# Two-layer graph network, attention layer: zero matmuls on TensorE behind each group's opening matmul, transposes over two PSUM banks instead of three

## The chip, the cores and the metric

The kernel runs on one core of a Trainium2 chip. The core has TensorE (PE; its weight loads are listed as PEld), VectorE (DVE), ScalarE (ACT), GpSimd (POOL) and SyncE (SP), each with its own instruction stream. The streams meet at semaphores. The metric is the time of one execution on the device in microseconds. Profiles are of one execution, taken by the hardware profiler.

## The reference, cut to what matters

There are 6250 nodes with 16 features and 206250 edges sorted by target node, each with 16 edge features and one of 230 types. Layer 0 is a relational message layer with hyperbolic maps. Layer 1, the attention layer, is the one that the change touches:

```python
w_m = (efeat @ W_msg + b_msg).reshape(E, in_f, -1)     # E x 16 x 16
w_a = (efeat @ W_attn + b_attn).reshape(E, in_f, -1)
h_src = feat[src][:, :, None]
e1 = w_m * h_src
e2 = w_a * h_src
seg_max = jax.ops.segment_max(e2, dst, num_segments=N)
ex = jnp.exp(e2 - seg_max[dst])
denom = jax.ops.segment_sum(ex, dst, num_segments=N)
attn = ex / denom[dst]
ft = jax.ops.segment_sum(e1 * attn, dst, num_segments=N)
return ft.sum(axis=1)
```

All matrices and sums are in float32. Edge features and weights are split into three bfloat16 parts, so that one bfloat16 matmul with a contraction over 100 rows gives a float32 product.

## The kernel before, in words

**Windows.** Nodes are ordered by degree and laid out 128 to a group, one node to a partition. A group with nodes of more than 48 edges takes several windows. Each window holds up to `S` = 48 edge slots for each of its 128 nodes. There are 50 windows here, run two at a time in a loop (`for q in range(2)`). A text that says "group" means one such pass. A window has up to eight blocks of `BLK` = 6 slots, and each block two halves of `HALF` = 3 slots. `nh` is the number of halves that a window really has, `nb` that of its blocks. Later windows have fewer.

**One window, engine by engine.** Work of window k and k+1 overlaps.

- GpSimd gathers the source features h by indirect DMAs (L325), one for each slot. For window k+1 it also fetches the edge features, and makes the second and third bfloat16 part of them (`residue`, L376; `last_part`, L380).
- TensorE, score phase: `weights(0, ...)` (L490) multiplies transposed edge features `efT` by the attention weights into one of two halves of `psW`. Between these, `exp_sums` (L496) adds the exponentials of the window before into the left half of the bank `psS`. `close_sums` (L504) ends the accumulation of the window before.
- TensorE, middle: the first two halves of the message weights, then `transposes(k + 1)` (L484): 48 transposes of edge features in six batches of 8, each batch into one bank of `psT`, which ScalarE copies to `efT` (`copies`, L620). A batch waits until ScalarE has copied the batch that used its bank before. Then TensorE waits until VectorE has read the sums of the window before (`sum_read`), and opens the new sums with a matmul of zeros of 1 row x 512 columns (L529).
- TensorE, message phase: `weights(IO, ...)` (L490) for halves 2 and later, and per block, when VectorE has put the products into `stage` (`q_ready`), `prod_sums` (L501) and a closing zero matmul (L542) that frees the ring slot (`q_free`, a ring of 3).
- VectorE, score phase: `scores(b)` multiplies `psW` by the gathered h (L1049, output in `arena`) and keeps the running maximum (L1061, L1065, L1068), then reduces it (L1070). Then `finish` for the window before: it reads `psS` (L1011), releases it, takes the reciprocal (L1013) and writes the output row (L1017).
- VectorE, message phase: `messages(b)` subtracts the maximum (L1089), multiplies the message weights in `psW` by h (L1049, output in `stage`), waits for ScalarE's exponential of the block (L637, L641), and multiplies the two (L1099).
- ScalarE: splits the edge features (L611, L614), makes the six copies of window k+1 (L620), one small exponential (L633), and the exponentials of the blocks of window k (L637), in this order.

The order on each engine is written out by hand. There is no planner. `psW` fills four PSUM banks, `psS` one, `psT` three. The third bank of `psT` (its columns 8 to 11 of 12) is also used once by the plan of windows ahead of layer 1, and by the transposes of layer 0 at the start (L430), which keep three banks.

Of the kernel before, what the change touches and what calls it, by code (L numbers as in the profile page):

```python
# [19 lines left out]
GP = 128  # L20
# [5 lines left out]
S = BLK * NBW  # L26
# [10 lines left out]
KE = 6 * D + 4  # L37
HI, MID, LO = 0, 3 * D, 5 * D
RING = 3
# [17 lines left out]
def build(nc, x, src, dst, efeat, etype, relw, loopw, relemb, wmsg, bmsg, wattn, battn, out, scratch):  # L57
    table_d, srcp_d, pairp_d, efp_d, h2_d, first_d, info_d = scratch
    ctx = ExitStack()
    with ctx:  # L60
        def sb(name, shape, dt=F32):
            return ctx.enter_context(nc.sbuf_tensor(name, shape, dt))

        def sem(name):
            return ctx.enter_context(nc.semaphore(name))
# [35 lines left out]
        efs = stage[0:GP, o2:o2 + S * KE // 2].bitcast(BF16).rearrange("p (s k) -> p s k", k=KE)  # L101
        o2 += S * KE // 2
        efT = stage[0:KE, o2:o2 + S * GP].bitcast(BF16).rearrange("k (q s n) -> k q s n", q=2, n=GP)
# [39 lines left out]
        identb = sb("identb", [128, 128], BF16)  # L143
        tri = sb("tri", [PN, PN])
        ones = sb("ones", [GP, GP])
        zero = sb("zero", [1, 512], BF16)
# [39 lines left out]
        psW = ctx.enter_context(nc.psum_tensor("psW", [128, 2, 1024], F32))  # L186
        psS = ctx.enter_context(nc.psum_tensor("psS", [128, 512], F32))
        psT = ctx.enter_context(nc.psum_tensor("psT", [128, 12, 128], F32))
        psTb = psT[:, :, :].rearrange("p a n -> p (a n)").bitcast(BF16).rearrange("p (t s n) -> p t s n", t=3, n=128)

        names = ("x_in dst_in edges_in relw_in wts_in wzero pads_ready const var_ready std_ready htan_ready hT_ps hT_sb "
# [9 lines left out]
        m = {n: sem("s_" + n) for n in names}  # L201
# [11 lines left out]
        def window(eng, k):  # L213
            v = eng.value_load(tabgn[:, ds(k, 1)], min_val=0, max_val=GC * GSTEP + GSTEP - 1)
            return v // GSTEP, (v % GSTEP) // 4 + 1
# [5 lines left out]
        def blocks(nh):  # L221
            return (nh + 1) // 2
# [48 lines left out]
        def _(pool):  # L271
# [57 lines left out]
            with pool.Fori(0, pairs) as i:  # L329
                for q in range(2):  # L330
                    k = 2 * i + q
                    _, ns = window_slots(pool, k)
                    pool.wait_ge(m["blk_in"], 16 * k + 16)
                    pool.wait_ge(m["l0_math"], k + 1)
                    pool.sem_inc(m["passed"], 1)
                    for b in range(MINS):
                        gather(table_d, blkidx, q, b, 1, tgath)
                    if q:
                        pool.wait_ge(tgath[0], pool.snap(cum[0]) * 16)
                        pool.sem_inc(m["passed"], 1)  # L340
                    else:
                        with pool.If(i > 0):
                            pool.wait_ge(tgath[1], pool.snap(cum[1]) * 16)
                            pool.sem_inc(m["passed"], 1)
                    pair_block(k + 1, 1 - q)
                    with ExitStack() as deeper:
                        for b in range(MINS, S):
                            deeper.enter_context(pool.If(ns > b))
                            gather(table_d, blkidx, q, b, 1, tgath)
                    pool.reg_add(cum[q], cum[q], ns)  # L350
# [72 lines left out]
        def _(pe):  # L423
            pe.wait_ge(m["const"], 2)
            pe.wait_ge(m["htan_ready"], 1)
            for t in range((C + 7) // 8):
                if t >= 3:
                    pe.wait_ge(m["hT_sb"], t - 2)
                for j in range(min(8, C - 8 * t)):
                    last = nc.tensor.transpose(psTb[0:KT, t % 3, j, 0:PN], htan6[:, 8 * t + j, :, :].rearrange("p j k -> p (j k)"),  # L430
                                               identb[0:PN, 0:PN])
# [32 lines left out]
            with pe.Fori(0, nstep) as t:  # L464
                pe.wait_ge(m["win_hot"], t + 1)
                for j, rhs in ((0, winhot), (1, winhot), (2, winrel)):
                    last = nc.tensor.matmul(psT[0:GP, 4 * j:4 * j + 4, :].rearrange("p a n -> p (a n)"), lhs[:, j, :],
                                            rhs, start=True, stop=True)
# [9 lines left out]
            def transposes(w):  # L478
                pe.wait_ge(m["lo_done"], w + 1)
                pe.wait_ge(m["valid_in"], w + 1)  # L480
                for t in range(S // 8):
                    pe.wait_ge(m["efT_sb"], w * (S // 8) + (t + 1))
                    for j in range(8):
                        last = nc.tensor.transpose(psTb[0:KE, t % 3, j, 0:GP], efs[:, 8 * t + j, :], identb[0:GP, 0:GP])  # L484
                    last.then_inc(m["efT_ps"], 1)

            def weights(c0, q, h, at0):
                pe.wait_ge(m["w_free"], at0 + (h + 1))
                for j in range(HALF):
                    last = nc.tensor.matmul(psW[0:GP, h % 2, j * IO:(j + 1) * IO], efT[:, q, h * HALF + j, 0:GP],  # L490
                                            wst[:, c0:c0 + IO], start=True, stop=True)
                last.then_inc(m["w_ready"], 1)

            def exp_sums(q, h):
                for s in range(h * HALF, (h + 1) * HALF):
                    nc.tensor.matmul(psS[0:GP, 0:IO], ident[0:GP, 0:GP], score[:, q, s, :], start=False, stop=False)  # L496

            def prod_sums(h):
                for s in range(HALF):
                    c0 = (h % (2 * RING) * HALF + s) * IO  # L500
                    nc.tensor.matmul(psS[0:GP, IO:2 * IO], ident[0:GP, 0:GP], prod[:, c0:c0 + IO], start=False, stop=False)  # L501

            def close_sums():
                nc.tensor.matmul(psS[0:GP, :], zero[:, 0:GP], zero[:], start=False, stop=True).then_inc(m["sum_done"], 1)  # L504

            transposes(0)
            with pe.Fori(0, pairs) as i:
                for q in range(2):
                    k = 2 * i + q
                    _, nh = window(pe, k)  # L510
                    nb = blocks(nh)
                    tb, prev = pe.snap(cumb), pe.snap(nhp)
                    pe.wait_ge(m["efT_sb"], k * (S // 8) + (S // 8 + 3))

                    for h in range(NHW):
                        if h < MINH:
                            weights(0, q, h, tb * 4)
                        else:
                            with pe.If(nh > h):
                                weights(0, q, h, tb * 4)  # L520
                        with pe.If(prev > h):
                            exp_sums(1 - q, h)
                    with pe.If(prev > 0):
                        close_sums()
                    for h in range(2):
                        weights(IO, q, h, tb * 4 + nb * 2)
                    transposes(k + 1)
                    pe.wait_ge(m["sum_read"], k + 1)
                    nc.tensor.matmul(psS[0:GP, :], zero[:, 0:GP], zero[:], start=True, stop=False)  # L529
                    for b in range(NBW):  # L530
                        for h in range(2 * b + 2, min(2 * b + 4, NHW)):
                            if h < MINH:
                                weights(IO, q, h, tb * 4 + nb * 2)
                            else:
                                with pe.If(nh > h):
                                    weights(IO, q, h, tb * 4 + nb * 2)
                        with pe.If(nb > b):
                            pe.wait_ge(m["q_ready"], tb + (b + 1))
                            prod_sums(2 * b)
                            with pe.If(nh > 2 * b + 1):  # L540
                                prod_sums(2 * b + 1)
                            nc.tensor.matmul(psS[0:GP, IO:2 * IO], zero[:, 0:GP], zero[:, 0:IO], start=False,  # L542
                                             stop=False).then_inc(m["q_free"], 1)
                    pe.reg_add(cumb, cumb, nb)
                    pe.reg_mov(nhp, nh)
            prev = pe.snap(nhp)
            for h in range(NHW):
                with pe.If(prev > h):
                    exp_sums(1, h)
            close_sums()  # L550


        @block.scalar
        def _(act):
# [8 lines left out]
            for t in range((C + 7) // 8):  # L563
                n = min(8, C - 8 * t)
# [26 lines left out]
            with act.Fori(0, pairs) as i:  # L591
                for q in range(2):
                    k = 2 * i + q
# [23 lines left out]
            def copies(w, q):  # L617
                for t in range(S // 8):
                    act.wait_ge(m["efT_ps"], w * (S // 8) + (t + 1))
                    nc.scalar.copy(efT[:, q, 8 * t:8 * t + 8, 0:GP], psTb[0:KE, t % 3, :, 0:GP]).then_inc(m["efT_sb"], 1)  # L620

            split(0)
            copies(0, 0)
            with act.Fori(0, pairs) as i:
                for q in range(2):
                    k = 2 * i + q
                    split(k + 1)
                    copies(k + 1, 1 - q)
                    _, nh = window(act, k)
# [16 lines left out]
        def _(dve):  # L646
            V = nc.vector

            for name, n in (("tbl_sb", 2), ("l0_math", 2), ("h_free", 2), ("efT_sb", 3), ("w_free", 2), ("q_free", RING),
                            ("sum_read", 1)):  # L650
                dve.sem_inc(m[name], n)
            V.memset(relW[:, RO:RO + D], 0.0)
# [215 lines left out]
            start = info[:, :, 2 * D]  # L868
# [18 lines left out]
            with dve.Fori(0, pairs) as i:  # L887
                for q in range(2):
                    k = 2 * i + q
# [138 lines left out]
            with dve.Fori(0, pairs) as i:  # L1028
                for q in range(2):
                    k = 2 * i + q  # L1030
# [3 lines left out]
                    last, odd = (nh - 1) // 2, nh % 2  # L1034
# [100 lines left out]
```

## Time and profile before

| | us |
|---|---|
| median of 3 runs (lowest to highest) | 6593.14 (6592.74 to 6606.66) |
| profiled execution | 6588.29 |
| its span, first to last instruction | 6586.6 |

Busy time over the span: TensorE 2729.8 us (41%), its weight loads 1922.8 us (29%), VectorE 3678.9 us (56%), ScalarE 1293.7 us (20%), GpSimd 4382.1 us (67%). Mean granted TensorE clock 0.92 of full speed. These shares run over two layers with different limits: layer 0 ends near 3050 us, layer 1 takes the rest. In a row, "[0.33 <-issue]" is the idle time of the engine just before it and what ended it, where "issue" is nothing that the profile shows and "remote" is something the profile cannot name. "x6" is a number of instructions shown as one line. A name like `psW<-wst,stage` is output, arrow, inputs.

### The profile page before, as it was taken

To read this page: it belongs to the slowest core of one execution; us is meant where nothing else is said; L and a number is where in the kernel's file an instruction comes from. 1 tells how busy PE (TensorE), PEld (TensorE's weight loads), DVE (VectorE), ACT (ScalarE), POOL (GpSimd) and SP (SyncE) were. 2 spreads that over 40 slices of the span, in tenths; PEclk is the share of its full clock that TensorE was granted. 3 is DMA by queue.
4 is the path that set the end of the run, shared out by engine and by line. 5 is a ranking of instruction groups with operands and counts; after the bars stand their busy time and mean duration, and the time that the engine had idled before them with its cause. 6 is when DMAs were issued, how large, how long until landed. Compare 5 with 4: busy or idle time off the path is not lost.

```text
span 6586.6 us, 56916 instructions
## 1 busy us (share of the span) xinstructions
PE 2729.8 (41%) x13477; PEld 1922.8 (29%) x13478; DVE 3678.9 (56%) x4670; ACT 1293.7 (20%) x1247; POOL 4382.1 (67%) x3814
## 2 busy tenths in 40 slices
PE   3530000000000000000567777777777777777676
PEld 1110000000000000000445555555555555555454
DVE  8221111111112111231689989998988898888877
ACT  3530000000000000000222222222222222223222
POOL 0335676767666766656477877777777777776753
PEclk9999999999999999998788888888888888888888
DMA  5880000000000000000000000000000000000000
GB/s 164 275 263 11 6 6 6 6 6 6 6 6 6 6 6 6 6 8 11 6 10 10 12 9 9 9 9 12 9 9 12 9 12 9 12 12 9 12 11 5
DMA packets 141814, 167.76 MB, mean 25 GB/s; under 512 B 73235, under 2 KB 130056, under 8 KB 135287
## 3 DMA queue, kind: packets, MB, share of 16 engines
q0 software_dynamic: 122896, 57.46, 6.2%
q1 hardware_dynamic: 18865, 110.05, 5.2%
q8 instruction: 8, 0.13, 0.0%
q14 instruction: 13, 0.11, 0.0%
q10 hardware_dynamic: 32, 0.01, 0.0%
HBM read 71.76 MB, written 108.57 MB: 27 GB/s over the span
## 4 chain that ended last, share of the span: by engine, by line
POOL 23%; issue 18%; DVE 17%; DVEq 16%; PE 13%; DMA 4%; another core or an unknown queue 4%; POOLq 2%; ACT 1%; SPq 0%; ACTq 0%
POOL gath L325 20%; DVEq L1096 6%; PE psS L501 4%; PE psS L496 4%; DVE stage L1049 4%; PE psW L490 3%; DMA table<-arena 3%; DVEq L1057 3%; DVE arena L1049 2%; DVE work L1070 2%; DVEq L1049 1%; DVE stage L1099 1%; DVE work L673 1%; DVE work L1013 1%
## 5 line engine op out<-in xcount | busy, mean ns | idle before, releaser
L325 POOL DMA_INDIRECT gath<-h_dram,hidx x1695 | 2223.5, 1312 | 509.3 <-issue 509.1
L325 POOL DMA_INDIRECT gath<-table,blkidx x1646 | 1600.0, 972 | 505.7 <-issue 503.0
L484 PE MATMUL psT<-identb,stage 128*100 128x128 bf16 x2448 | 209.5, 255 | 2599.5 <-POOL stage L380 2569.7
L501 PE MATMUL psS<-stage,ident 128*128 128x256 f32 x3390 | 976.3, 447 | 341.8 <-DVE stage L1099 297.7
L484 PEld LDWEIGHTS psT<-identb,stage 128*100 128x100 bf16 x2448 | 190.8, 155 | 2623.9 <-POOL stage L380 2531.5
L501 PEld LDWEIGHTS psS<-stage,ident 128*128 128x128 f32 x3390 | 736.5, 225 | 534.3 <-DVE stage L1099 354.0
L496 PE MATMUL psS<-arena,ident 128*128 128x256 f32 x3390 | 830.4, 382 | 0.0
L490 PE MATMUL psW<-wst,stage 100*128 100x256 bf16 x3390 | 580.0, 292 | 472.2 <-DVE stage L1049 270.0
L673 DVE TENSOR_TENSOR work<-gath 128x768 f32<-128x768 f32 x50 | 47.9, 958 | 1154.1 <-DMA gath<-table,blkidx 1150.8
L496 PEld LDWEIGHTS psS<-arena,ident 128*128 128x128 f32 x3390 | 605.5, 191 | 70.2
L1049 DVE TENSOR_TENSOR arena<-psW,gath 128x768 f32 (+1 forms) x565 | 520.7, 952 | 173.8 <-DMA gath<-h_dram,hidx 58.2
L637 ACT ACTIVATE arena<-arena x271 | 401.9, 1483 | 1019.3 <-DVE arena L1089 989.4
L1099 DVE TENSOR_TENSOR stage<-stage,arena x294 | 498.6, 1696 | 88.7 <-issue 35.3
L620 ACT COPY stage<-psT 100x1024 bf16<-100x1024 bf16 x306 | 289.9, 1026 | 1298.8 <-PE psT L484 1213.6
L1049 DVE TENSOR_TENSOR stage<-psW,gath 128x768 f32 x565 | 513.9, 949 | 24.8 <-remote 24.8
L1089 DVE TENSOR_TENSOR arena<-arena,work 128x1536 f32 (+1 forms) x294 | 496.8, 1690 | 16.2 <-issue 16.2
L490 PEld LDWEIGHTS psW<-wst,stage 100*128 100x128 bf16 x3390 | 287.2, 101 | 725.5 <-DVE stage L1049 325.8
L595 ACT ACTIVATE work<-work 128x48 f32<-128x48 f32 x50 | 12.1, 243 | 2236.7 <-DVE work L905 2092.1
L1065 DVE TENSOR_TENSOR work<-work,arena 128x1536 f32<-128x1536 f32 x171 | 328.6, 1922 | 15.8
L874 DVE SCALAR_TENSOR_TENSOR bstf<-tabs,info 128x1 f32 (+1 forms) x103 | 21.7, 211 | 472.0 <-issue 472.0
L446 PE MATMUL psW<-stage,work 102*125 102x460 bf16 (+1 forms) x400 | 190.9, 617 | 173.1 <-ACT arena L578 141.4
L376 POOL TENSOR_TENSOR efraw<-efraw,stage 128x768 f32<-128x768 f32 x51 | 86.3, 1692 | 236.2 <-DVEq L1000 173.7
(216 smaller groups left out, 2680.3 us busy)
## 6 DMA issues: line engine op xcount, KB each, us to landing
table<-arena SPq DMA_DIRECT2D x50, 1610.0 KB
gath<-h_dram,hidx POOLq DMA_INDIRECT x1695
gath<-table,blkidx POOLq DMA_INDIRECT x1646
efp<-in_edge_attr SPq DMA_DIRECT2D x1, 12890.6 KB
table<-arena SPq DMA_DIRECT2D x50, 186.9 KB
arena<-first_dram POOLq DMA_DIRECT2D x1, 915.5 KB, 12.1
info<-info_dram POOLq DMA_DIRECT2D x2, 432.0 KB, 6.4
arena<-in_dst,rowi POOLq DMA_INDIRECT x51
```

The lines of the kernel that those rows point to most:

```text
L325: pool.indirect_dma_start(out=gath[:, q, s, :], out_offset=None, in_=rows, in_offset=bass.IndirectOffsetOnAxis(ap=idx[:, q, s:s + 1].bitca ...
L484: last = nc.tensor.transpose(psTb[0:KE, t % 3, j, 0:GP], efs[:, 8 * t + j, :], identb[0:GP, 0:GP])
L490: last = nc.tensor.matmul(psW[0:GP, h % 2, j * IO:(j + 1) * IO], efT[:, q, h * HALF + j, 0:GP], wst[:, c0:c0 + IO], start=True, stop=True)
L496: nc.tensor.matmul(psS[0:GP, 0:IO], ident[0:GP, 0:GP], score[:, q, s, :], start=False, stop=False)
L501: nc.tensor.matmul(psS[0:GP, IO:2 * IO], ident[0:GP, 0:GP], prod[:, c0:c0 + IO], start=False, stop=False)
L620: nc.scalar.copy(efT[:, q, 8 * t:8 * t + 8, 0:GP], psTb[0:KE, t % 3, :, 0:GP]).then_inc(m["efT_sb"], 1)
L637: nc.scalar.activation(v, v, ACT.Exp).then_inc(m["exp_done"], 1)
L1049: V.tensor_tensor(dst_ap.rearrange("p s (i o) -> p s i o", o=D), psW[0:GP, s, 0:HALF * IO].rearrange("p (s i o) -> p s i o", i=D, o=D), bc ...
L1065: V.tensor_tensor(macc, macc, score[:, q, ds(b * BLK, BLK), :], ALU.max)
L1089: V.tensor_tensor(blk, blk, mnew[:, q, :].unsqueeze(1).to_broadcast([GP, n, IO]), ALU.subtract).then_inc(m["sub_done"], 1)
L1096: V.drain()
L1099: V.tensor_tensor(pr, pr, blk.rearrange("p s c -> p (s c)"), ALU.mult).then_inc(m["q_ready"], 1)
```

## The change

TensorE gets a helper that writes a matmul of zeros (1 row by 128, times 1 row by 512 columns) into a spare bank n times. It is called with 12 behind the opening matmul of the sums in each window, ahead of the message phase. The spare bank is the third one of `psT`. So that it is free, the batches of transposes in layer 1 alternate between two banks instead of three, in TensorE's writes and in ScalarE's reads alike. The start value of the semaphore that counts copied batches goes from 3 to 2, and so does the constant in the wait at the head of a window, which still waits for the last copy of that window.

```diff
         psT = ctx.enter_context(nc.psum_tensor("psT", [128, 12, 128], F32))
+        spare = psT[0:GP, 8:12, :].rearrange("p a n -> p (a n)")
...
                 for t in range(S // 8):
                     pe.wait_ge(m["efT_sb"], w * (S // 8) + (t + 1))
                     for j in range(8):
-                        last = nc.tensor.transpose(psTb[0:KE, t % 3, j, 0:GP], efs[:, 8 * t + j, :], identb[0:GP, 0:GP])
+                        last = nc.tensor.transpose(psTb[0:KE, t % 2, j, 0:GP], efs[:, 8 * t + j, :], identb[0:GP, 0:GP])
                     last.then_inc(m["efT_ps"], 1)
...
+            def keep_busy(n):
+                for _ in range(n):
+                    nc.tensor.matmul(spare, zero[:, 0:GP], zero[:], start=True, stop=True)
...
-                    pe.wait_ge(m["efT_sb"], k * (S // 8) + (S // 8 + 3))
+                    pe.wait_ge(m["efT_sb"], k * (S // 8) + (S // 8 + 2))
...
                     transposes(k + 1)
                     pe.wait_ge(m["sum_read"], k + 1)
                     nc.tensor.matmul(psS[0:GP, :], zero[:, 0:GP], zero[:], start=True, stop=False)
+                    keep_busy(12)
...
-                    nc.scalar.copy(efT[:, q, 8 * t:8 * t + 8, 0:GP], psTb[0:KE, t % 3, :, 0:GP]).then_inc(m["efT_sb"], 1)
+                    nc.scalar.copy(efT[:, q, 8 * t:8 * t + 8, 0:GP], psTb[0:KE, t % 2, :, 0:GP]).then_inc(m["efT_sb"], 1)
...
-            for name, n in (("tbl_sb", 2), ("l0_math", 2), ("h_free", 2), ("efT_sb", 3), ("w_free", 2), ("q_free", RING),
+            for name, n in (("tbl_sb", 2), ("l0_math", 2), ("h_free", 2), ("efT_sb", 2), ("w_free", 2), ("q_free", RING),
```

## Rows read from the trace of the kernel before

**Rows 1.** Page, part 2: VectorE's busy tenths in 40 equal slices.

```profile
DVE  8221111111112111231689989998988898888877
```

**Rows 2.** Windows of layer 1: stretch, length, busy (count) of PE, PEld, DVE, ACT, POOL; clock, DMA.

```profile
3400.00:4900.00 1500.00, 1120.21 (x5825) 820.26 (x5824) 1347.86 (x1382) 399.81 (x329) 1171.33 (x871) 0.88 0.06 10
4900.00:6500.00 1600.00, 1170.36 (x6007) 865.65 (x6007) 1383.76 (x1496) 451.00 (x376) 1165.87 (x887) 0.84 0.07 11
```

**Rows 3.** Timeline of VectorE, one group's message phase: start us, duration us, instruction.

```profile
5036.33 1.76 DVE L1089 TENSOR_TENSOR arena<-arena,work 128x1536 f32 x1 [0.33 <-issue]
5038.01 1.82 DVE L1049 TENSOR_TENSOR stage<-psW,gath 128x768 f32 x2
5039.92 1.76 DVE L1099 TENSOR_TENSOR stage<-stage,arena  x1
...
5043.26 1.81 DVE L1049 TENSOR_TENSOR stage<-psW,gath 128x768 f32 x2
```

**Rows 4.** Timeline of TensorE in the same group.

```profile
5032.68 0.38 PE L529 MATMUL psS<-zero 1*128 1x512 bf16 x1 [1.37 <-DVEq L1012]
5039.02 1.68 PE L490 MATMUL psW<-wst,stage 100*128 100x256 bf16 x6 [5.96 <-DVE stage L1049]
5041.73 5.49 PE L501 MATMUL psS<-stage,ident 128*128 128x256 f32 x12 [1.03 <-DVE stage L1099]
...
5047.36 0.83 PE L490 MATMUL psW<-wst,stage 100*128 100x256 bf16 x6
5048.03 2.75 PE L501 MATMUL psS<-stage,ident 128*128 128x256 f32 x12
```

**Rows 5.** Windows around the same gap; the clock is third from the end.

```profile
5033.00:5039.00 6.00, 0.06 (x1) 0.00 (x0) 5.43 (x8) 2.12 (x4) 4.69 (x5) 0.54 0.05 6
5039.00:5048.00 9.00, 7.91 (x25) 5.11 (x26) 8.82 (x7) 2.21 (x2) 7.31 (x5) 0.55 0.05 5
5048.00:5067.00 19.00, 15.43 (x75) 11.27 (x73) 17.55 (x17) 7.66 (x6) 15.39 (x11) 1.00 0.05 5
```

**Rows 6.** Waits after 3400 us: who waited for whom, us in total, times, longest.

```profile
DVE arena L1049 <- PE psW L490: 53.3, 89, 2.7
...
DVE stage L1099 <- issue: 35.3, 6, 9.4
...
DVE stage L1099 <- ACT arena L637: 10.9, 6, 5.2
...
DVE stage L1049 <- remote: 3.6, 3, 2.9
```

**Rows 7.** Source line L529: duration ns min/median/max, first and last start.

```profile
L529 PE MATMUL psS<-zero x50: 384/385/605, 3162.2 to 6533.7; 1*128 1x512 bf16 x50
```

**Rows 8.** Windows around the first group's transposes in the loop.

```profile
3157.00:3160.00 3.00, 3.00 (x30) 2.87 (x31) 2.90 (x2) 1.30 (x2) 0.00 (x0) 0.57 0.00 0
3160.00:3164.00 4.00, 2.11 (x26) 1.44 (x24) 3.63 (x4) 4.00 (x5) 0.00 (x0) 1.00 0.01 4
```

**Rows 9.** Timeline of the first group: six copies, and the fifth batch of transposes.

```profile
3158.70 5.58 ACT L620 COPY stage<-psT 100x1024 bf16<-100x1024 bf16 x6 [46.02 <-PE psT L484]
...
3160.68 0.65 PE L484 MATMUL psT<-identb,stage 128*100 128x128 bf16 x8 [0.18 <-ACT stage L620]
```

**Rows 10.** Timeline of ScalarE: the first block exponential of the group of rows 3.

```profile
5038.24 1.48 ACT L637 ACTIVATE arena<-arena  x1 [2.67 <-issue]
```

**Rows 11.** Timeline of a later group, 6162 to 6196 us.

```profile
6166.03 4.81 PE L484 MATMUL psT<-identb,stage 128*100 128x128 bf16 x48 [3.38 <-POOL stage L380]
...
6174.50 1.68 PE L490 MATMUL psW<-wst,stage 100*128 100x256 bf16 x6 [3.34 <-DVE stage L1049]
...
6174.76 1.01 ACT L620 COPY stage<-psT 100x1024 bf16<-100x1024 bf16 x1 [4.76 <-remote]
...
6181.99 1.01 ACT L620 COPY stage<-psT 100x1024 bf16<-100x1024 bf16 x1 [3.27 <-remote]
...
6184.73 1.76 DVE L1099 TENSOR_TENSOR stage<-stage,arena  x1 [9.42 <-issue]
```

## The prediction, made before the changed kernel was run

> **What bounds the kernel now.** I read the page's slices first. VectorE has 1 to 3 tenths in slices 3 to 18 (counted from 0), which are layer 0, and 7 to 9 tenths from slice 20 on, which is layer 1 [rows 1]. The edit touches layer 1 alone. Next the windows of that layer: from 3400 to 4900 us VectorE is busy 1347.86 of 1500 us, TensorE 1120.21, GpSimd 1171.33, and the granted clock is 0.88; in the next 1600 us they have 1383.76, 1170.36 and 1165.87, and 0.84 [rows 2]. The clock has two levels, 2.4 and 1.2 GHz, so 0.88 means that 24% of the time is at the lower one.
>
> Then one group of nodes (window of 48 edge slots), around 5033 to 5067 us, engine by engine. VectorE starts the first message block at 5036.33 (subtract), multiplies by h at 5038.01, makes the product at 5039.92, and reaches the second block's multiply at 5043.26 [rows 3]. None of these lines has an idle time in front except 0.33 us of issue. 5043.26 - 5038.01 = 5.25 us is one block and is 1.76 + 1.82 + 1.76 us of instructions, less overlaps. TensorE in the same time: the opening matmul of the sums (L529) at 5032.68, then 5.96 us of idle, which VectorE ends by giving psW back, then weights at 5039.02 in 1.68 us and the first 12 sums in 5.49 us. The next block's weights take 0.83 and its 12 sums 2.75 us [rows 4]. The windows say why: 0.54 of the clock from 5033 to 5039, 0.55 from 5039 to 5048, 1.00 afterwards [rows 5]. That is 2 x (0.46 x 6 + 0.45 x 9) = 13.6 us at 1.2 GHz per group. TensorE pays some 3.6 us for it (0.85 + 2.74), and VectorE's 5.25 us beat doesn't change. So the question is who waits for the slow TensorE.
>
> The waits answer it. Of VectorE's waits after 3400 us, the multiplies into `stage` (message blocks) have 3.6 us in 3 waits. The multiplies into `arena` (scores, on the far side of the group) have 53.3 us in 89 waits. The product waited for the exponential: 35.3 us in 6 waits and 10.9 in 6 [rows 6]. Layer 1 is VectorE bound, and the slow clock after the gap lies beside it.
>
> **The change part by part.**
>
> (a) Twelve matmuls of zeros. L529 ran 50 times, so 50 groups, 600 matmuls of 1 x 512. The trace has none of them back to back. Upper bound: L529 alone takes 0.385 us, at worst 0.605 [rows 7], so 12 x 0.605 = 7.3 us with no overlap. Lower bound: six 256-column matmuls in 0.83 us [rows 4], where the last one ends 0.28 after its start, so (0.83 - 0.28) / 5 = 0.11 us each, 0.22 for 512 columns, 2.6 us for twelve. At 1.2 GHz that doubles to 5.3. I take 2.6, since L529's own median of 0.385 us is near its minimum of 0.384, the full clock's [rows 7]. They stand between L529 and the weights for half 2. The gap is 5.96 us [rows 4], so 2.6 and 5.3 both fit. At 7.3 the weights start 1.3 us late; they are first read at 5043.26, and now end at 5040.70, which leaves 2.6 us more. So VectorE pays 0 at all three prices. What hides it is VectorE's own tail of `finish` and the first subtract. If that cover were gone, it would be 2.6 x 50 = 130 us.
>
> (b) The clock. After the zeros an idle time of about 5.96 + 0.38 - 2.6 - 0.3 = 3.4 us is left. Idle pieces that add up to 3.6 us over 19 leave the clock at 1.00 (5048 to 5067), 6 us in one piece do not [rows 4, 5]. 3.4 in one piece lies between; I take it that the clock still falls in most groups, but some 4 us later, and comes back where it did. So 13.6 becomes about 9.5 us per group; L529 runs from 3162.2 to 6533.7 in 49 steps [rows 7], which is 68.8 us from group to group, and so the mean clock gains 0.5 x 4 / 69 = 0.03, from 0.88 and 0.84 to about 0.90 and 0.87. If it never fell, it would be +0.10. Value in time: at most the 3.6 us of `stage` waits [rows 6], and nothing below that.
>
> The row bears on a rule: in the first group the mean clock was 0.57 from 3157 to 3160, which are transposes nearly throughout, so the low level and the rise lie both in them, and 1.00 up to 3164 [rows 8]. The Trainium skill (TensorE: Matmul & The Clock Gate, Part 4: PE-mode transpose) says that the full clock doesn't engage for transposes, which don't count as busy in the same way. By that rule, which speaks against this change, the zeros would find the clock already low and cost 5.3 us a group instead of 2.6, and do little for it; the row contradicts it, since the clock rose during transposes.
>
> (c) Transposes over two banks. There are six batches of 8 a group, each copied out by ScalarE. In the first group the six copies stand in 5.58 us, thus (5.58 - 1.03) / 5 = 0.91 us apart, and the fifth batch waited 0.18 us for a copy and took 0.65 [rows 9]. With two banks a batch waits for the copy one later, so the last ends 0.9 us later. On TensorE this eats into the wait before L529, or at worst pushes it by 0.9; hidden as in (a). On ScalarE two copies take 1.82 us; one copy plus one batch is 1.03 + 0.65 + some 0.1 = 1.8 at the full clock, no loss, and 1.03 + 1.06 + 0.1 = 2.2 at half clock (batch of 8 x 0.107 plus 0.2 fill, worked out from 0.65), so 0.2 a copy, 1.0 a group. ScalarE idles 2.67 us before the first exponential [rows 10], so this is free too, except where the product already waits for the exponential: 12 times [rows 6]. 12 x 1.0 = 12 us at most; I take 5.
>
> Those twelve have an own face. Around 6174 us all 48 transposes ended by 6170.84, yet the fourth copy started 4.76 us late at 6174.76 and the sixth at 6181.99, so VectorE's product stood idle 9.42 us until 6184.73 [rows 11]. The matmuls had ended but their increments came late. With two banks the sixth batch waits for the fourth copy, that is until 6175.8, and its increment follows. Bounds for this: nothing (the increments come when they come) to one further lag of 4.8 us in each of the six long waits, 29 us. I take 3. The weights at 6174.50 [rows 11] would be up to 6 us late there, while VectorE needs them about 3.5 us after 6184.73: hidden.
>
> (d) 24 more instructions in each of two unrolled loop bodies. TensorE's first pass through new code shows only as waits that no engine ends; one bound is the 3.6 us row, the other nothing: I take 1. The start value of the copy semaphore and the wait at the group's head drop by one together; the wait is for the same copy. 0.
>
> Sum on the profiled execution: 6588.3 + 0 - 1 + 5 + 3 + 1 = 6596. The page's span is 6586.6, its run 6588.3, and the median 6593.1, 4.8 higher. I forecast the median: 6593 + 8 = 6601; as (c) takes the upper half of what is likely, I shade it to 6598.
>
> **The rivals.**
>
> Slower (late increments compound): with two banks each late copy now holds TensorE, whose next increment is late in its turn. It decides where the fourth copy is late, as in rows 11. For it: in rows 11 the copies after the fourth are late again, up to 6181.99. Against: 6 of 50 groups show it at this size. Price: the full 12 + 29 us and the zeros at 5.3 us behind: 6593 + 41 = 6634.
>
> Faster (ScalarE no longer late): late increments of this kind might belong to a TensorE at 1.2 GHz; the six weights at 6174.50 took 1.68 us, which is that level [rows 4, 11]. If a clock that holds removes them, VectorE gets back its 35.3 + 10.9 us [rows 6]: 6593 - 46 = 6547. Against: the transposes come before the zeros.
>
> Nothing happens to the clock: a matmul with one row of zeros isn't counted as work. Then (b) is 0 and the mean clock stays at 0.88 and 0.84; the time is 6593 to 6601, since nothing waits for it. The clock held throughout gives the same time.
>
> **How the numbers follow.** About 0.2% (13 us) is what can be told from no change. Forecast 0.45, the clock unchanged or held 0.13, slower rival 0.24, faster rival 0.18. The first two end within 13 us of 6593 but for a tenth of them, mostly upwards. So same 0.51, slower 0.29, faster 0.20. The range goes down to 6560 and up to 6640 to take most of both rivals; the forecast's own range is 6588 to 6612.
>
> **What would show it.** Right: groups of twelve matmuls on `psT` about 2.6 us long behind L529; VectorE's beat of 5.25 us unchanged; mean clock up by 0.02 to 0.04; copies 0.91 us apart at the full clock; the `stage` multiplies still waiting a few us in all. Wrong: waits for psW in front of the second message block (then (a) isn't hidden), the product's waits for the exponential well above 50 us or gone, or a mean step from one L529 to the next off 68.8 us by over 0.3.

## The result, and the profile after

| | before | changed |
|---|---|---|
| median of 20 runs (lowest to highest), us | 6575.64 (6555.76 to 6606.66) | 6618.9 (6582.34 to 6665.19) |
| profiled execution, us (before: the one of the first table) | 6588.29 | 6605.61 |

The ratio is 1.0063, 95% interval 1.0045 to 1.0080: the changed kernel is slower. The median of before had been 6593.14 over three runs and is 6575.64 over twenty. Measured again beside the experiments below, on a chip where the kernel before is 29 us quicker (chip B), the same changed kernel gave 1.0027 (1.0012 to 1.0042), 6558.54 against 6546.22 us. So the loss is 0.3 to 0.6%, 18 to 41 us by the two ratios.

The windows of layer 1 in the trace of the changed kernel answer to [rows 2]; the clock is third from the end:

```profile
3400.00:4900.00 1500.00, 1208.32 (x6128) 852.45 (x6126) 1355.66 (x1395) 397.68 (x323) 1179.86 (x876) 0.90 0.07 10
4900.00:6500.00 1600.00, 1269.40 (x6310) 896.66 (x6309) 1379.61 (x1500) 452.64 (x376) 1158.45 (x884) 0.85 0.06 11
```

TensorE is busier by 88 and 99 us, VectorE is as before. The clock went from 0.88 to 0.90 and from 0.84 to 0.85. One group, TensorE's timeline, answers to [rows 4]. L534 is the old L529, L506 are the zeros, L491 and L502 the old L490 and L501:

```profile
5241.61 0.38 PE L534 MATMUL psS<-zero 1*128 1x512 bf16 x1
5241.84 2.75 PE L506 MATMUL psT<-zero 1*128 1x512 bf16 x12
5247.75 1.69 PE L491 MATMUL psW<-wst,stage 100*128 100x256 bf16 x6 [3.16 <-DVE stage L1055]
5250.46 5.16 PE L502 MATMUL psS<-stage,ident 128*128 128x256 f32 x12 [1.03 <-issue]
5255.56 0.28 PE L548 MATMUL psS<-zero 1*128 1x256 bf16 x1
5255.77 0.83 PE L491 MATMUL psW<-wst,stage 100*128 100x256 bf16 x6
```

The zeros take 2.75 us and the weights behind them still wait 3.16 us for VectorE, so they don't start late. They still take 1.69 us, and the first twelve sums 5.16: the half clock is back before the messages begin. VectorE in the same group answers to [rows 3]. The second block's multiply stands at 5252.62, 5.88 us behind the first instead of 5.25:

```profile
5246.74 1.82 DVE L1055 TENSOR_TENSOR stage<-psW,gath 128x768 f32 x2
5248.65 1.76 DVE L1105 TENSOR_TENSOR stage<-stage,arena  x1
5250.32 1.75 DVE L1095 TENSOR_TENSOR arena<-arena,work 128x1536 f32 x1
5252.62 1.82 DVE L1055 TENSOR_TENSOR stage<-psW,gath 128x768 f32 x2 [0.54 <-remote]
```

Its weights had ended on TensorE at 5249.44, 3.2 us earlier. The increment that tells of them came late. The waits after 3400 us, against [rows 6], show more of this kind of wait: 22 of them for `stage` where there were 3.

```profile
DVE arena L1055 <- PE psW L491: 46.0, 75, 2.7
DVE stage L1105 <- issue: 32.2, 6, 8.0
...
DVE stage L1055 <- remote: 18.4, 22, 3.5
DVE stage L1105 <- ACT arena L643: 6.5, 6, 1.2
```

Ahead of 3400 us there is one more long one, in the second group. The sixth copy started 15.81 us late, though its transposes had ended at 3245.09, and VectorE's product stood idle 30.15 us:

```profile
3244.00 1.09 PE L485 MATMUL psT<-identb,stage 128*100 128x128 bf16 x8 [1.83 <-issue]
...
3245.42 5.32 PE L506 MATMUL psT<-zero 1*128 1x512 bf16 x12
...
3266.16 1.01 ACT L626 COPY stage<-psT 100x1024 bf16<-100x1024 bf16 x1 [15.81 <-remote]
...
3268.89 1.76 DVE L1105 TENSOR_TENSOR stage<-stage,arena  x1 [30.15 <-issue]
```

That group isn't where the two traces part, though. In the same group the kernel before has 33.8 us of such waits (12.5 for the exponential, 21.3 for `stage`), the changed kernel 37.6 (30.1 and 7.5). They part in the third group. The opening matmuls of the fourth stand 24.4 us apart (before, then changed), where those of the third stood 3.2 us apart:

```profile
3412.71 0.38 PE L529 MATMUL psS<-zero 1*128 1x512 bf16 x1 [1.50 <-DVEq L1012]
3437.11 0.38 PE L534 MATMUL psS<-zero 1*128 1x512 bf16 x1 [0.57 <-DVEq L1018]
```

In between the changed kernel waits three times for `stage`, and once for the exponential for 5.1 us. The kernel before has 1.4 us for the exponential there and no wait for `stage`:

```profile
DVE stage L1055 <- remote: 16.5, 3, 11.2
```

From there to the last opening matmul the changed kernel is 5.8 us quicker (3115.2 us against 3121.0). Its 14.8 us more of `stage` waits after 3400 us are made up by 7.3 us less for scores and 7.7 us less for the exponential. So this pair of executions differs by 17.3 us, all of it by one early group, and doesn't show a price that is paid in every group.

### The profile page after: what moved, and what is told of

Same layout as the page of the kernel before. It is cut to its first block, busy times and chain, and to the rows that moved or that the text cites. A ratio compares the mean times of both kernels' runs of the same rounds, so it can differ in the third digit from the quotient of the medians.

```text
span 6603.8 us, 58116 instructions
## 1 busy us (share of the span) xinstructions
PE 2937.5 (44%) x14077; PEld 1989.3 (30%) x14078; DVE 3676.3 (56%) x4670; ACT 1299.8 (20%) x1247; POOL 4372.0 (66%) x3814
## 4 chain that ended last, share of the span: by engine, by line
POOL 24%; issue 19%; DVEq 17%; DVE 16%; PE 13%; DMA 4%; another core or an unknown queue 3%; POOLq 2%; ACT 1%; SPq 0%; ACTq 0%
POOL gath L326 21%; DVEq L1102 6%; DVE stage L1055 4%; PE psS L502 4%; PE psS L497 4%; PE psW L491 3%; DMA table<-arena 3%; DVEq L1063 3%; DVE arena L1055 2%; DVE work L1076 2%; DVEq L1055 1%; DVE work L679 1%; DVE work L1019 1%; DVE stage L1105 1%
## 5 line engine op out<-in xcount | busy, mean ns | idle before, releaser
L485 PE MATMUL psT<-identb,stage 128*100 128x128 bf16 x2448 | 231.1, 257 | 2658.6 <-issue 2543.6
L502 PE MATMUL psS<-stage,ident 128*128 128x256 f32 x3390 | 974.5, 446 | 304.8 <-DVE stage L1105 238.9
L502 PEld LDWEIGHTS psS<-stage,ident 128*128 128x128 f32 x3390 | 735.8, 225 | 499.2 <-DVE stage L1105 291.4
L491 PE MATMUL psW<-wst,stage 100*128 100x256 bf16 x3390 | 578.0, 291 | 295.7 <-DVE arena L1055 112.7
L491 PEld LDWEIGHTS psW<-wst,stage 100*128 100x128 bf16 x3390 | 286.5, 101 | 570.2 <-DVE arena L1055 200.4
```

The source lines that it names most:

```text
L485: last = nc.tensor.transpose(psTb[0:KE, t % 2, j, 0:GP], efs[:, 8 * t + j, :], identb[0:GP, 0:GP])
```

## The experiments

Twelve kernels ran, on three chips, each beside runs of the kernel before on the same chip: e1 to e4 on chip A (before: 6548.32 us), e5 to e8 on chip B (6546.22) and e9 to e12 on chip C (6574.9). Which chip the first measurement (6575.64) was taken on isn't known.

| run | what differs | ratio to before | 95% |
|---|---|---|---|
| first measurement | the change | 1.0063 | 1.0045 to 1.0080 |
| e5 | the change, chip B | 1.0027 | 1.0012 to 1.0042 |
| e1 | two banks alone | 1.0002 | 0.9993 to 1.0011 |
| e4, e7 | two banks alone, as it turned out | 1.0005, 1.0004 | 0.9996 to 1.0014, 0.9994 to 1.0015 |
| e2 | twelve zeros alone, three banks | 1.0025 | 1.0012 to 1.0039 |
| e8 | the change, zeros of 16 columns | 1.0035 | 1.0022 to 1.0048 |
| e6 | the change, 100 rows of weights for the row of zeros | 1.0024 | 1.0015 to 1.0033 |
| e9 | code of the 12 zeros present, jumped over | 1.0025 | 0.9998 to 1.0051 |
| e3 | 24 zeros | 1.0339 | 1.0325 to 1.0354 |
| e10 | code of 24 zeros present, jumped over | 1.0266 | 1.0236 to 1.0296 |
| e11 | 36 zeros of 16 columns from a loop | 1.0623 | 1.0577 to 1.0669 |
| e12 | before, fewer closing matmuls | 1.0015 | 0.9993 to 1.0037 |

**e1_banks_only.**

```diff
-                    keep_busy(12)
```

> The change without the zero matmuls: the layer 1 transposes alternate between two banks of psT, nothing is written to the third. Theory A (late copies compound): the two banks carry the loss, so the ratio to the kernel before is 1.004 to 1.008, and ScalarE's copies show more late starts and VectorE's product (message phase) waits 15 us or more longer than the 60 us it waits before. Theory B (the zeros carry it, through increments of TensorE that arrive late or weights that start late): ratio 0.998 to 1.002. Theory C (longer code in the loop bodies): also 0.998 to 1.002, since this loop is as long as before.

Measured: 6550.45 us, 1.0002. VectorE's product waited 44.4 us for the exponential in this trace after 3200 us (65.0 in that of the kernel before), not more. Theory A falls on this chip: the two banks cost nothing that can be told.

**e2_zeros_only.**

```diff
 nc.tensor.matmul(psS[0:GP, :], zero[:, 0:GP], zero[:], start=True, stop=False)
+for _ in range(12):
+    nc.tensor.matmul(psS[0:GP, :], zero[:, 0:GP], zero[:], start=False, stop=False)
```

> Three banks for the transposes as before, and behind the opening matmul of psS in each window twelve more matmuls of zeros of 1 x 512 into psS itself, accumulating, so they need no spare bank. Theory A: ratio 0.998 to 1.002, waits of VectorE's product as before. Theory B: 1.004 to 1.008. Theory C: 1.002 to 1.006. The granted clock in layer 1 should be as in the changed kernel, 0.01 to 0.04 above the kernel before, in all three.

Measured: 6565.06 us, 1.0025, which is under B's bound of 1.004 and within C's. The whole change gives 1.0027 on chip B (e5, below). Beside the 1.0002 of e1, the zeros carry the loss on these two chips, and no compounding with the banks can be told.

**e3_change_24.**

```diff
-                    keep_busy(12)
+                    keep_busy(24)
```

> The change with 24 zero matmuls in place of 12. At the full clock they take 5.2 us, which nearly fills the gap of 6 us, so the clock should mostly hold: mean granted clock in layer 1 0.93 or more, the first twelve sums of a message block 2.75 us instead of 5.5. Theory A: ratio as the change, 1.004 to 1.008, since the banks are the same. Theory B: doubled, 1.009 to 1.016, with VectorE's multiplies into stage waiting 50 us or more longer. If a clock that holds were worth time by itself, the ratio would fall below 1.003.

Measured: 6768.4 us, 1.0339. All theories missed it, and so did the clock. The 24 zeros back to back don't hold it; it is at the lower level right through them:

```profile
3995.31 10.44 PE L506 MATMUL psT<-zero 1*128 1x512 bf16 x24
4005.69 1.46 PE L491 MATMUL psW<-wst,stage 100*128 100x256 bf16 x6
```

The windows over that stretch, with TensorE busy throughout:

```profile
3995.00:4000.00 5.00, 5.00 (x12) 1.64 (x13) 4.45 (x6) 1.44 (x3) 3.78 (x5) 0.50 0.06 6
4000.00:4006.00 6.00, 6.00 (x16) 2.01 (x15) 5.37 (x5) 1.88 (x2) 5.08 (x4) 0.50 0.04 4
```

Over 47 groups the clock fell during the zeros in 38 and was already low in 9; in none did it hold. The time went somewhere else. The page's line of instruction fetches says 224 packets, where the kernel before and the changed one have 8:

```profile
q8 instruction: 224, 3.67, 0.3%
```

TensorE's branch back to the head of the loop took 4.2 to 4.9 us in 23 passes, so every second window began late, and VectorE waited for scores (`arena`) at the cold start:

```profile
5285.76 0.82 PE L491 MATMUL psW<-wst,stage 100*128 100x256 bf16 x3 [5.57 <-issue]
```

```profile
DVE arena L1055 <- PE psW L491: 161.5, 142, 3.8
```

**e4_code_not_run** and **e7_long_code_not_run.**

```diff
-                    keep_busy(12)
+                    with pe.If(nh > 100):
+                        keep_busy(12)     # 24 in e7
```

> The change with its twelve zero matmuls under a condition that is never true, so their code lies in both loop bodies but doesn't run; two banks as in the change. Theory A: the same ratio as the two banks alone. Theory B: as the two banks alone, 0.998 to 1.002. Theory C: 1.004 to 1.008 here, and above the two banks alone by that much. The branch itself costs TensorE well under 1 us a window and lies beside VectorE.

> 24 zero matmuls as in the run with 24, but under a condition that is never true, so that only their code is there. With 24 executed, TensorE's branch back to the loop's head took 4.2 to 4.9 us in all of the 23 passes after 3400 us, and 224 instruction packets were fetched instead of 8. Theory L (the loop body no longer fits where TensorE keeps its code): the same packets and the same branch here, and a ratio of 1.02 to 1.035. Theory B (24 executed zeros in front of the message weights cost it): 1.000 to 1.002.

Measured: 6553.23 us, 1.0005, and 6551.48 us, 1.0004, with 8 packets. The bound of `nh` is known when the kernel is compiled, so I take it that the zeros weren't in either program. e7's 8 packets bear this out: the same 24 matmuls under a condition on a running count take 224 (e10, below). Both are repeats of e1, and say nothing of the code.

**e5_change_again.** The changed kernel as it is.

> The changed kernel itself, beside the others of this call on one chip. The two banks alone gave 1.0002, the zeros into psS with three banks 1.0025, the code without its execution 1.0005. Theory B (the zeros' execution costs, the banks nothing): 1.002 to 1.004, that is, part of the first measurement's 1.0063 was its chip. Theory D (zeros and two banks compound, since each late increment now holds the next transposes too): 1.005 to 1.008 again.

Measured: 6558.54 us, 1.0027: B's figure, and D falls here. The first measurement's 1.0063 lies in D's range, and beside it neither part was run alone. The profiled execution took 6545.17 us, at the low end of its runs, and has few of the late increments (9 waits for `stage`, 3.4 us), so its trace can't show where the typical run loses its 12 us.

**e6_hundred_rows.**

```diff
-                    nc.tensor.matmul(spare, zero[:, 0:GP], zero[:], start=True, stop=True)
+                    nc.tensor.matmul(spare, wst[:, 0:GP], wst[:], start=True, stop=True)
```

> The change with the twelve idle matmuls made from 100 rows of the weights (100 x 128 times 100 x 512, written to the spare bank) instead of one row of zeros; same count, same columns, same code length. With one row the clock fell while they ran back to back, 0.22 us apart before and 0.43 behind. If the clock's fall depends on how many rows of the array work, it holds through these twelve, they are 0.22 us apart in nearly all groups, and the low stretch behind the gap gets some 3 us shorter than with the change (mean clock in layer 1 up by 0.02 more). If it doesn't depend on rows or data, the spacing is as in the change. The time: within 0.2% of the change by theory B, since VectorE sets the pace; a ratio at or under 1.000 only if the half clock behind the gap is what makes the increments late.

Measured: 6559.68 us, 1.0024. The twelve ran at the full clock from first to last in 24 of 47 groups and the clock fell during them in 8, where the change in e5 has 10 and 20. In the 16 us behind the opening matmul the clock is low for some 8.3 us; with the zeros 11.2 (11.4 in e5), in the kernel before 12.5. The two banks without any zeros have 11.3 as well (e1 and e7), so the one-row zeros took nothing off the half clock: what the change shows against the kernel before, the banks alone show too. The windows of [rows 2] now read:

```profile
3400.00:4900.00 1500.00, 1212.03 (x6068) 857.52 (x6066) 1358.88 (x1383) 402.20 (x326) 1187.70 (x873) 0.90 0.07 10
4900.00:6500.00 1600.00, 1254.51 (x6346) 892.58 (x6346) 1384.78 (x1506) 452.44 (x375) 1148.36 (x874) 0.89 0.07 11
```

So rows or data matter to the clock (this run doesn't part the two), and a third less of the half clock than in the kernel before, a quarter less than with the banks alone, is worth no time.

**e8_narrow_zeros.**

```diff
-                    nc.tensor.matmul(spare, zero[:, 0:GP], zero[:], start=True, stop=True)
+                    nc.tensor.matmul(spare[:, 0:16], zero[:, 0:GP], zero[:, 0:16], start=True, stop=True)
```

> The change with twelve zero matmuls of 1 x 16 columns instead of 1 x 512: as many instructions, but under 0.7 us of TensorE's time instead of 2.6 to 5.3. If the loss comes from the number of instructions that TensorE completes (its increments late behind them), the ratio stays as for the change in this call, within 0.1%. If it comes from the time that the zeros take, it falls to 1.000 to 1.001.

Measured: 6571.26 us, 1.0035. Twelve now take 0.46 us of TensorE instead of 4.2 on average, and the loss is as large. It isn't TensorE's time that costs; it is that the instructions are there, run or only in the code (e9 tries to part these two).

**e9_code_12_skipped** and **e10_code_24_skipped.**

```diff
-                    keep_busy(12)
+                    with pe.If(tb > 5000):
+                        keep_busy(12)     # 24 in e10
```

> The change with its twelve zero matmuls under a condition on the running block count that is never true and that the compiler can't fold away, so that 24 more instructions really lie in each loop body and are jumped over. (The two earlier kernels with a condition on nh turned out to be compiled without the zeros: they are repeats of the two banks alone, at 1.0005 and 1.0004.) Theory N (TensorE completes more instructions and its increments come later): 0.999 to 1.001. Theory C (longer code): 1.002 to 1.004, as the change and the narrow zeros (1.0027, 1.0035).

> The same with 24 zero matmuls skipped. With 24 executed the ratio was 1.0339, 224 instruction packets were fetched instead of 8, and the branch back to the loop's head took 4.2 to 4.9 us. If the length of the code alone does that: 150 packets or more, the same branch times, ratio 1.015 to 1.03. If fetched code is only what runs: 8 packets and 1.000 to 1.001.

Measured: e9 6599.27 us, 1.0025 (0.9998 to 1.0051), which holds both theories and doesn't part them. Its trace has no wait for `stage` after 3400 us, like those of e4 and e7. e10 6758.7 us, 1.0266, with 224 packets and the branch at 4.3 to 5.1 us. So the length of the loop alone (with one jump a window, and on chip C) makes 2.7%, where e3 has 3.4. The trace shows the same late scores:

```profile
q8 instruction: 224, 3.67, 0.2%
```

```profile
DVE arena L1056 <- PE psW L491: 186.8, 148, 3.9
```

**e11_loop_36_narrow.**

```diff
-                    keep_busy(12)
+                    with pe.Fori(0, 6) as _z:
+                        keep_busy(6)      # of 1 x 16 columns
```

> 36 zero matmuls of 1 x 16 columns in each window, from a loop of 6 passes over 6 of them, so that only about half of the change's instructions are added to the code but three times as many run. TensorE needs some 2 to 3 us for them, less than the gap of 6 us. Theory N (number of completed instructions): 1.006 to 1.011, three times the narrow zeros' 1.0035 or at least twice. Theory C (length of the code): 1.001 to 1.002. If neither, and the loss is a matter of chance in how the streams fall, it lies between 1.000 and 1.003.

Measured: 6981.18 us, 1.0623, far above all three. 8 packets, so it isn't the fetch. The timeline of one group shows TensorE going through 31 of the 36 in 1.96 us, and then stalling with nothing to wait for in front of each further one. Over the 50 groups the first stall of more than half a microsecond comes behind 18 to 35 zeros; 17 groups have none.

```profile
5258.75 1.96 PE L506 MATMUL psT<-zero 1*128 1x16 bf16 x31
5261.48 0.17 PE L506 MATMUL psT<-zero 1*128 1x16 bf16 x1 [0.77 <-issue]
5262.93 0.17 PE L506 MATMUL psT<-zero 1*128 1x16 bf16 x1 [1.29 <-issue]
5264.38 0.17 PE L506 MATMUL psT<-zero 1*128 1x16 bf16 x1 [1.27 <-issue]
5265.80 0.17 PE L506 MATMUL psT<-zero 1*128 1x16 bf16 x1 [1.26 <-issue]
5267.23 0.17 PE L506 MATMUL psT<-zero 1*128 1x16 bf16 x1 [1.26 <-issue]
5267.97 0.58 PE L491 MATMUL psW<-wst,stage 100*128 100x256 bf16 x2 [0.57 <-issue]
5268.71 1.13 PE L491 MATMUL psW<-wst,stage 100*128 100x256 bf16 x4 [0.16 <-issue]
...
5277.85 0.96 DVE L1056 TENSOR_TENSOR stage<-psW,gath 128x768 f32 x1 [8.67 <-remote]
```

The weights ended at 5269.84 and VectorE, idle since 5269.18, could read them at 5277.85. There are 94 such waits in 47 windows:

```profile
DVE stage L1056 <- remote: 337.7, 94, 10.9
```

338 us of VectorE's waits against 406 us of added time: this is the kind of wait of the changed kernel's trace, 18 times as long. Here it comes behind 48 transposes and 36 zeros in a few us, each with a weight load. Against e8, three times as many zeros and the inner loop with its branches came in together, so this run doesn't show which of the two brings the stalls; 36 narrow zeros without a loop weren't run.

**e12_fewer_closing.**

```diff
-                                prod_sums(2 * b + 1)
-                            nc.tensor.matmul(psS[0:GP, IO:2 * IO], zero[:, 0:GP], zero[:, 0:IO], start=False,
-                                             stop=False).then_inc(m["q_free"], 1)
+                                prod_sums(2 * b + 1, free=True)    # its last matmul increments q_free
+                            with pe.If(nh < 2 * b + 2):
+                                nc.tensor.matmul(psS[0:GP, IO:2 * IO], zero[:, 0:GP], zero[:, 0:IO], start=False,
+                                                 stop=False).then_inc(m["q_free"], 1)
```

> The kernel before with fewer TensorE instructions: where a block has both halves, the zero matmul of 1 x 256 columns that closes it and frees its ring slot is left out, and the last product sum does the increment instead. Some 5 matmuls and weight loads fewer per window, one branch more per block. Theory N: the ratio falls below 1, to 0.997 to 0.9995, with fewer waits of VectorE on late increments. Theory C: 0.999 to 1.001, as the code has grown by a few branches. VectorE's beat of 5.25 us stays in both.

Measured: 6582.91 us, 1.0015 (0.9993 to 1.0037). No gain that can be told; the interval leaves theory N 0.07% at most. The kernel before had only 3 waits for `stage` after 3400 us, this one has 2, so there was hardly a late increment to free. No version here is faster than the kernel before.

**The traces side by side.** One execution each. `stage` waits are VectorE's with releaser "remote" after 3400 us. The step is the mean time from one opening matmul to the next, from the fourth to the fiftieth.

| trace | chip | `stage` waits, us | step, us |
|---|---|---|---|
| before | first measurement | 3, 3.6 | 67.85 |
| the change | first measurement | 22, 18.4 | 67.72 |
| e1, e4: two banks alone | A | 0, 0 | 67.05, 67.11 |
| e2: zeros alone | A | 4, 2.0 | 67.35 |
| e7: two banks alone | B | 0, 0 | 67.10 |
| e5: the change | B | 9, 3.4 | 67.09 |
| e6: the change, 100 rows | B | 18, 9.8 | 67.64 |
| e8: the change, narrow zeros | B | 12, 4.8 | 67.27 |

Over the 46 steps, 0.3 us is 14 us. So in e2, e6 and e8 the later groups do carry a loss of the size that the medians show (8 to 25 us against the banks alone on the same chip), and in e5's trace and in that of the first measurement they don't.

## Why the prediction was right or wrong

The time fell inside the range (6560 to 6640) but not in its likeliest case: I gave 0.51 to no change and 0.29 to slower, and it was slower both times. The forecast was 5 us over the median then known for the kernel before; measured side by side it is 41 us by the ratio, or 18 on chip B. The range took that in through the room that I had left for the rivals, not through a term of the sum. That the slower rival's price was 41 us too is luck: its banks cost nothing that can be told where they ran alone.

1. What bounds the kernel: right. VectorE's beat stays at 5.25 us where no increment is late, and e6 has a third less half clock for no gain.
2. (a) The zeros lie in TensorE's gap: right as to TensorE (2.75 us at the full clock against 2.6 foretold, 5.32 at the half, 3.96 on average in the changed kernel's trace). The step that failed is "VectorE pays 0 at all three prices": the bounds counted TensorE's time alone. What the runs showed instead: by the medians the twelve cost 12 us in e5, 25 us in e8 with a ninth of TensorE's time, and 17 us in e2 without the banks. So the price hangs on the instructions being there. Through which wait it is paid is open. Late increments for `stage`, which I had listed under (c) only, are more frequent with zeros and two banks together (9 to 22 waits) than with the banks alone (none) or in the kernel before (3). But e2 has the loss with 4 of them and 2.0 us, so they aren't all of it: against e1 on the same chip its trace has 8.8 us more for the exponential and 5.1 us more for scores, in one execution each.
3. (b) The clock: the 0.90 for the first stretch was hit, the second was 0.85 and not 0.87. The hit is luck. Another execution of the same kernel (e5) has 0.88 and 0.86, and the two banks without zeros have 0.89 and 0.86 (e1). I had the clock fall in the 3.4 us of idle left behind the zeros; in 19 of 47 groups it fell while they ran, and in e3 24 of them didn't hold it either. The third rival's premise, that one row of zeros isn't counted as work, was nearer, and its conclusion, that time doesn't care, holds by e6. [rows 8] have the clock rise within a run of transposes, and a batch of eight takes 0.65 us in [rows 9] against 1.09 at the half clock (at 3244.00 above). The Trainium skill (TensorE: Matmul & The Clock Gate, Part 4: PE-mode transpose) says that the full clock doesn't engage for transposes. These rows contradict it. They don't show that transposes alone raise it: six weight matmuls ended at 3157.81, just before the rise.
4. (c) Two banks: foretold +8 us, measured by three runs at 1.0002, 1.0005 and 1.0004, or +1 to +3 us, none of them clear of zero. The slower rival had the sign, and the late increments right in kind. That they compound with the banks shows in the number of `stage` waits (point 2) and not in the time: e2 without the banks is as slow as e5 with them. Beside the first measurement, with its larger loss, this is untested.
5. (d) Longer loop bodies: foretold 1 us, and only for the first pass. I didn't ask how much room was left. With 12 zeros the loop is still fetched once; with 24 it is fetched again in every pass for 2.7%.
6. The faster rival: nothing of it showed. The copies were as late as before: counted from the end of their transposes or of ScalarE's instruction before, 68 late starts with 119 us in all in the changed kernel's trace against 53 with 98.
7. Of the signs of being wrong one came: the mean step from one opening matmul to the next was 69.2 us, 0.4 over 68.8. From the fourth group on it was 67.7, against 67.9 in the kernel before, so this sign speaks of the third group and not of the rest.

What stays open: which waits make up the 0.3% of the twelve, and whether they come from running the zeros or from the code's length (e9 can't part them, and e12 found no gain from fewer instructions); why the loss is 0.6% in the first measurement and 0.3% on chip B, where the kernel before is 29 us quicker too; and what holds TensorE's increments back.

## What to carry to other kernels

An instruction that fills an idle engine isn't free because its time is hidden: twelve narrow matmuls of 0.46 us in all cost as much here as twelve wide ones. Ask also what the instructions add to the loop's code. And before a trace is taken to show the loss, look in which groups the two traces part: in the pair shown it was one early group, and executions of the changed kernel on one chip spread over 58 us (e5), more than the loss. Before keeping a clock up, ask who waits for the slow engine; here nobody did, and matmuls with one row of zeros didn't keep it up either.

## What the runs showed of the hardware that I had not expected

- Matmuls with one row of zeros, back to back for 10.4 us, ran at 1.2 GHz to the end (0.50 granted from 3995 to 4006). With 100 rows of weights twelve of them kept 2.4 GHz in 24 of 47 groups, with one row of zeros in 10 (e5). Zeros in all rows weren't tried.
- With 24 more matmuls a window, each with its weight load (96 instructions in the two windows of a pass), TensorE's loop body was fetched anew in each pass: 224 packets of instructions for 8, and a branch of 4.2 to 5.1 us, even where the added code was jumped over. With 12 more a window there were 8 packets.
- 24 matmuls under a condition that can be decided when the kernel is compiled took 8 packets, under one that can't 224, so the first kind can't stand for code that is present but not run.
- After 48 transposes and 31 narrow zeros, each with its weight load, TensorE stalled about 1.3 us in front of each further matmul in the group shown, and the increment of finished weights reached VectorE 8 us late (e11).
